# Mixed tokens of 26 tiles kept as fp32, their fp16 halves made in front of the pairs, low rank product in fp32

## The reference

```python
x = x + L0_ffn(L0_cond(x, cond, ...))   # grouped conv of 9 taps + bias; int8 matmul, int32 sums, two scales, fp16
x = x + L1_ffn(L1_cond(x, cond, ...))
# L1_cond: att = softmax(mlp(cond)); out = einsum('boi,bih->boh', agg_w(att), x) + agg_b
# L1_ffn:  H = x W^T + b;  z = x A  (rank 32)
#          logits from H[:, odd tokens, :8] and (z LiMEs^T)[odd tokens], each over its largest magnitude
#          weights = softmax, masked by the second largest;  p_mix = repeat(weights, 2) LiMEs
#          out = H + (z * p_mix) Bmat * scaling
```

## Time and profile before

| | us |
|---|---|
| median of 3 runs | 648.18 |
| span of the profiled execution | 646.6 |
| TensorE busy | 623.8 |
| VectorE busy | 418.3 |
| ScalarE busy | 335.3 |
| GpSimd busy | 336.2 |

### The profile page before, as it was taken

The page is one execution under the profiler, slowest core; times in us unless marked ns, Lnnn a source line. Parts: engine busy times, 40 slices in busy tenths (PEclk is TensorE's granted clock), DMA queues, the critical chain, the costliest instruction groups (busy, mean ns, idle before and its releaser), DMA issues.

```text
span 646.6 us, 14948 instructions
## 1 busy us (share of the span) xinstructions
PE 623.8 (96%) x5865; PEld 337.3 (52%) x5898; DVE 418.3 (65%) x891; ACT 335.3 (52%) x566; POOL 336.2 (52%) x223
## 2 busy tenths in 40 slices
PE   7789999999999999999999999999999999999997
PEld 5556565566566666656554444444444444444443
DVE  5958778877787778787537797745544433444434
ACT  2857898667778777776652436334333313333100
POOL 3012222217778522225485689886866678666400
PEclk8799999999999999999999999999999999999999
DMA  8969877677799797764529014554555433457103
GB/s 299 361 137 365 295 284 273 233 266 276 280 342 336 285 359 280 259 229 140 217 73 357 35 34 153 206 203 156 196 195 193 158 132 136 162 197 259 66 1 130
DMA packets 46707, 138.38 MB, mean 214 GB/s; under 512 B 13180, under 2 KB 13468, under 8 KB 46465
## 3 DMA queue, kind: packets, MB, share of 16 engines
q1 hardware_dynamic: 41886, 120.65, 52.6%
q10 hardware_dynamic: 4752, 16.78, 6.4%
HBM read 89.13 MB, written 48.28 MB: 213 GB/s over the span
## 4 chain that ended last, share of the span: by engine, by line
PE 51%; DVE 1%; issue 0%; ACT 0%; DVEq 0%
PE ps L770 36%; PE ps L584 9%; PE ps L752 2%; PE ps L521 2%; PE ps L505 1%; PE ps L462 0%; PE ps L552 0%; DVE z_lo L1304 0%; DVE unscale L1441 0%; DVE ring L1293 0%; DVE yb L1245 0%; DVE zT L1306 0%; PE ps L555 0%; PE ps L730 0%; PE ps L493 0%
## 5 line engine op out<-in xcount | busy, mean ns | idle before, releaser
L1088 POOL TENSOR_TENSOR x<-x_in,f_both 128x512 f32<-128x512 f32 x64 | 74.0, 1157 | 195.9 <-DVE f_both L1277 195.9
L521 PE MATMUL ps<-wqT,yq_both 128*128 128x512 bf16 x479 | 113.2, 379 | 6.0 <-issue 4.6
L462 PE MATMUL ps<-x_ph,conv_w 64*64 64x256 f32 (+1 forms) x1024 | 98.2, 396 | 2.2 <-DMA conv_w<-in_conv_taps 2.0
L863 ACT ACTIVATE yv<-yb,yinv 128x128 f32<-128x128 f32 x256 | 78.0, 389 | 2.3 <-DVE yinv L1268 2.2
L902 ACT ACTIVATE ring<-ring,ratio 128x2048 f16<-128x2048 f16 x26 | 50.6, 1994 | 51.1 <-DVE wst L1537 14.1
L770 PE MATMUL ps<-ffn_wT,ring 128*128 128x512 f16 x312 | 71.6, 379 | 0.0
L462 PEld LDWEIGHTS ps<-x_ph,conv_w 64*64 64x64 f32 (+1 forms) x1024 | 51.1, 137 | 37.4 <-issue 14.2
L521 PEld LDWEIGHTS ps<-wqT,yq_both 128*128 128x128 bf16 x512 | 45.2, 97 | 48.4 <-issue 1.0
L1245 DVE TENSOR_TENSOR yb<-ps,ybias 128x1024 f32<-128x1024 f32 x32 | 39.1, 1223 | 41.1 <-PE ps L462 41.0
L584 PE MATMUL ps<-ffn_wT,ring 128*128 128x512 f16 x288 | 64.6, 379 | 0.0
L856 ACT ACTIVATE ring<-ps,t_up 128x512 f16<-128x512 f32 x64 | 40.5, 683 | 45.5 <-issue 38.1
(11 more groups left out here) (284 smaller groups left out, 1096.6 us busy)
## 6 DMA issues: line engine op xcount, KB each, us to landing
x_ph<-in_x_phases SPq DMA_DIRECT2D x32, 516.0 KB, 6.1
x_in<-in_x SPq DMA_DIRECT2D x32, 512.0 KB, 6.4
x_scratch<-x SPq DMA_DIRECT2D x32, 512.0 KB, 2.8
x_scratch<-ring SPq DMA_DIRECT2D x26, 512.0 KB, 4.1
ring<-x_scratch SPq DMA_DIRECT2D x26, 512.0 KB, 4.3
wst<-in_w_rows SPq DMA_DIRECT2D x12, 512.0 KB, 5.0
x_in<-x_scratch SPq DMA_DIRECT2D x12, 512.0 KB, 6.5
out<-x_in ACTq DMA_DIRECT2D x12, 512.0 KB, 3.6
```

Of the source, the lines that this page charges most:

```text
L462: return mm(ps_conv[o, g * 2 * MB:(g + 1) * 2 * MB], conv_w[k, g, w.start + o.start:w.start + o.stop], xp[k, g, :, view], start=first, sto ...
L521: last = mm(acc_bank(t, h), yqT[:, t % 2, p, :], wqT[:, p, h * HALF:(h + 1) * HALF], start=p == 0, stop=p == PH - 1)
L863: last = A(yv[:, s, :], yb[:, t % 2, s, :], ACT.Copy, scale=yinv[:, s:s + 1], bias=MAGIC)
L1088: g.tensor_tensor(x1[:, t % 2, s], x_in[:, t % 3, s], f16[:, s], ALU.add).then_inc(sem("x1_ready"), 1)
```

## The change

- Mixed tiles 0 to 25 are kept in the ring and in the scratch tensor as fp32 without a scale. ScalarE copies bank 2 (one instruction in place of two) and no longer waits for the tile's scale; VectorE copies bank 3 (`x2_out`), in front of `layer0(c-2, 0)`. `low` is gone for these tiles. The last six tiles are treated as before.
- Their rank product is made in fp32: 8 matmuls of 40 columns, alternately to partitions 0 and 64, against fp32 weights `z_f`, which ScalarE makes in two instructions before the loop. `rank_out` takes two instructions for two tiles.
- In the last stage `normalized` scales an fp32 tile in place, with the pair's inverse scale; ScalarE rounds the high halves needed (`x_high`: half of the second tile, all of the first) into buffers of their own, three pairs deep, and GpSimd makes the low ones (`x_low`). `x_sums` is gone, and `s_sums` works in the ring in place. `pair` waits for `x_low` where it waited for `normalized`, and `fetch_x2` from the seventh pair tile on waits for `s_low`, where it waited for the end of a pair's products.
- The program is built with a smaller scratch for DMA descriptors, which makes room for the new buffers.

```diff
+x2_sums = ring_flat.rearrange("p (s c t) -> p s c t", s=RING, c=NL)
...
+z_f = sb("z_f", [P, NL, ZR], F32)
+x_part = sb("x_part", [P, 2, L], F32)
...
 def t_home(q):
...
-def x_sum(i):
-    return (bias_b, wsum_b)[i]
+x_homes = ((x_part[:, 0, :], x_part[:, 1, :]), tuple(yb[:, i, :, :].rearrange("p n m -> p (n m)") for i in range(2)),
+           (bias_b[:, :], wsum_b[:, :]))
+
+def x_home(j, i):
+    return x_homes[j % 3][i].bitcast(F16).rearrange("p (a n) -> p a n", a=2)
+
+def x_tile(j, i):
+    return ring[:, x2_slot(RING + 2 * j + i), :]
...
     def save_x2(t):
-        wait(sp, "lo_ready", 2 * t + 2)
+        sp.wait_ge(sem("x2a_ready"), t + 1)
+        sp.wait_ge(sem("x2b_ready"), t + 1)
...
-            sp.wait_ge(sem("prod_ready"), 7 * ((n - 2 * RING) // 2 + 1))
+            sp.wait_ge(sem("s_lo_ready"), 2 * ((n - 2 * RING) // 2 + 1))
...
-        wait(pe, "lo_ready", 2 * t)
+        if t <= KEPT:
+            wait(pe, "x2a_ready", t)
+            wait(pe, "x2b_ready", t)
+        else:
+            pe.wait_ge(sem("lo_ready"), 2 * (t - KEPT))
...
     def rank_pair(t):
-        wait(pe, "lo_ready", 2 * t + 4)
+        if t < KEPT:
+            pe.wait_ge(sem("x2a_ready"), t + 2)
+            pe.wait_ge(sem("x2b_ready"), t + 2)
+        else:
+            pe.wait_ge(sem("lo_ready"), 2 * (t - KEPT) + 4)
...
+            pe.wait_ge(sem("z_f_ready"), 2)
...
+        if t < KEPT:
+            for k in range(NL):
+                o = 64 * (k % 2)
+                last = mm(rank[o:o + ZR, 0:2 * P], z_f[:, k, :], x2_sums[:, s:s + 2, k, :],
+                          start=k < 2, stop=k >= NL - 2, skip_group_check=True)
+            last.then_inc(sem("z_psum"), 1)
+            return
...
-    def x2_part(n, half):
-        return lambda a, k: x2_cols[:, x2_slot(n), a, 4 * half + k, :]
+    def x2_part(j, i, half):
+        return lambda a, k: x_home(j, i)[:, a, (4 * half + k) * P:(4 * half + k + 1) * P]
...
     def pair(j, deltas):
-        n1, n2 = RING + 2 * j, RING + 2 * j + 1
...
-        pe.wait_ge(sem("norm_ready"), 2 * j + 2)
+        pe.wait_ge(sem("x_lo_ready"), 2 * j + 2)
...
-        product(sum_a, x2_part(n1, 0), w_part_of(0, 0), True)
+        product(sum_a, x2_part(j, 0, 0), w_part_of(0, 0), True)
...
     def high(t, h):
...
-            wait(act, "t_ready", 2 * t + 2)
+            if t >= KEPT:
+                act.wait_ge(sem("t_ready"), 2 * t + 2)
...
+        if t < KEPT:
+            if h == 0:
+                A(x2_sums[:, t % RING, :, 0:CH], bank(2).rearrange("p (c t) -> p c t", c=NL), ACT.Copy).then_inc(sem("x2a_ready"), 1)
+            return
...
     def normalized(n):
...
-        act.wait_ge(sem("ratio_ready"), 1)
-        cols = x2_cols[:, s, :, :, :].rearrange("p h c t -> p (h c t)")
-        A(cols, cols, ACT.Copy, scale=ratio[:, t:t + 1]).then_inc(sem("norm_ready"), 1)
+        act.wait_ge(sem("pair_inv_ready"), 1)
+        A(ring[:, s, :], ring[:, s, :], ACT.Copy, scale=pair_inv[:, t:t + 1]).then_inc(sem("norm_ready"), 1)
+
+    def x_high(j):
+        act.wait_ge(sem("norm_ready"), 2 * j + 2)
+        if j == 1:
+            act.wait_ge(sem("gateT_psum"), 1)
+        if j == 2:
+            act.wait_ge(sem("gate_ready"), 1)
+        if j >= 3:
+            act.wait_ge(sem("prod_ready"), 7 * (j - 2))
+        for i, lo in ((1, HALF), (0, 0)):
+            A(x_home(j, i)[:, 0, lo:L], x_tile(j, i)[:, lo:L], ACT.Copy).then_inc(sem("x_hi_ready"), 1)
...
-            act.wait_ge(sem("s_sum_ready"), 6 * j + (4 if i else 6))
-            A(s_home(j, i)[:, :, 0, :], x_sum(i)[:, :].rearrange("p (s n) -> p s n", s=2), ACT.Copy).then_inc(sem("s_hi_ready"), 1)
+            act.wait_ge(sem("s_sum_ready"), 4 * j + (2 if i else 4))
+            A(s_home(j, i)[:, :, 0, :], x_tile(j, i).rearrange("p (s n) -> p s n", s=2), ACT.Copy).then_inc(sem("s_hi_ready"), 1)
...
+    A(z_f[:, :, 0:R], pk[:, PACK["a"]].rearrange("p (k r) -> p k r", k=NL), ACT.Copy, scale=s_up[:, 1:2]).then_inc(sem("z_f_ready"), 1)
+    A(z_f[:, :, R:ZR], pk[:, PACK["w8"]].rearrange("p (k r) -> p k r", k=NL), ACT.Copy, scale=s_up[:, 0:1]).then_inc(sem("z_f_ready"), 1)
...
+    x_high(1)
...
+    x_high(2)
...
-    def x_sums(j):
-        for i in range(2):
-            n = RING + 2 * j + i
-            pool.wait_ge(sem("norm_ready"), n - RING + 1)
-            wait(pool, "s_lo_ready", 2 * j)
-            if n == RING:
-                pool.wait_ge(sem("gate_ready"), 1)
-            hi, lo = (x2_cols[:, x2_slot(n), a, :, :].rearrange("p c t -> p (c t)") for a in range(2))
-            g.tensor_tensor(x_sum(i)[:, :], hi, lo, ALU.add).then_inc(sem("s_sum_ready"), 1)
+    def x_low(j):
+        for i, lo in ((1, HALF), (0, 0)):
+            pool.wait_ge(sem("x_hi_ready"), 2 * j + (1 if i else 2))
+            h = x_home(j, i)
+            g.tensor_tensor(h[:, 1, lo:L], x_tile(j, i)[:, lo:L], h[:, 0, lo:L], ALU.subtract).then_inc(sem("x_lo_ready"), 1)
...
     def s_sums(j):
-        pool.wait_ge(sem("s_sum_ready"), 6 * j + 2)
-        a, b = x_sum(0), x_sum(1)
+        pool.wait_ge(sem("x_lo_ready"), 2 * j + 2)
+        a, b = x_tile(j, 0), x_tile(j, 1)
...
-            wait(pool, "s_sum_ready", 6 * j + 2 + i)
+            wait(pool, "s_sum_ready", 4 * j + i)
...
     def s_low(j):
...
-            g.tensor_tensor(h[:, :, 1, :], x_sum(i)[:, :].rearrange("p (s n) -> p s n", s=2), h[:, :, 0, :], ALU.subtract).then_inc(sem("s_lo_ready"), 1)
+            g.tensor_tensor(h[:, :, 1, :], x_tile(j, i).rearrange("p (s n) -> p s n", s=2), h[:, :, 0, :], ALU.subtract).then_inc(sem("s_lo_ready"), 1)
...
+    def x2_out(t):
+        if t >= KEPT:
+            return
+        dve.wait_ge(sem("mix_ready"), 2 * t + 2)
+        if t >= RING:
+            dve.wait_ge(sem("z_psum"), (t - RING) // 2 + 1)
+            dve.wait_ge(sem(f"x2_moved{t % RING}"), 16 * (t // RING))
+        v.tensor_copy(x2_sums[:, t % RING, :, CH:2 * CH], bank(3).rearrange("p (c t) -> p c t", c=NL)).then_inc(sem("x2b_ready"), 1)
+
     def low(t, h):
-        wait(dve, "hi_ready", 2 * t + h + 1)
+        if t < KEPT:
+            return
+        wait(dve, "hi_ready", 2 * (t - KEPT) + h + 1)
...
     def rank_out(t):
+        if t < KEPT:
+            dve.wait_ge(sem("z_psum"), t // 2 + 1)
+            dve.wait_ge(sem("z_bias_ready"), t // 8 + 1)
+            cols = slice(t * P, (t + 2) * P)
+            link(v.tensor_tensor(z_lo[:, :], rank_bank(t)[64:ZW, 0:2 * P], zT[64:ZW, cols], ALU.add))
+            v.tensor_tensor(zT[0:ZR, cols], rank_bank(t)[0:ZR, 0:2 * P], z_lo[:, :], ALU.add).then_inc(sem("z_ready"), 2)
+            return
...
-            link(v.scalar_tensor_tensor(z_lo[:, :], rank_bank(t)[64:ZW, i * P:(i + 1) * P], t_down[64:ZW, t + i:t + i + 1], zT[64:ZW, cols],
+            link(v.scalar_tensor_tensor(z_lo[:, 0:P], rank_bank(t)[64:ZW, i * P:(i + 1) * P], t_down[64:ZW, t + i:t + i + 1], zT[64:ZW, cols],
...
-                                   z_lo[:, :], ALU.mult, ALU.add).then_inc(sem("z_ready"), 1)
+                                   z_lo[:, 0:P], ALU.mult, ALU.add).then_inc(sem("z_ready"), 1)
...
-        link(v.tensor_scalar(pair_inv[:, :].bitcast(I32), pair_down[:, :].bitcast(I32), -1.0, float(254 << 23), ALU.mult, ALU.add))
-        v.tensor_tensor(ratio[:, :], t_down[:, 0:KEPT], pair_inv[:, :], ALU.mult).then_inc(sem("ratio_ready"), 1)
+        v.tensor_scalar(pair_inv[:, :].bitcast(I32), pair_down[:, :].bitcast(I32), -1.0, float(254 << 23), ALU.mult, ALU.add).then_inc(sem("pair_inv_ready"), 1)
...
+        x2_out(c - 3)
```

More of the change, by code:

```diff
@@ L156, in program @@
         unscale = sb("unscale", [P, NT], F32)
-        z_lo = sb("z_lo", [ZR, P], F32)
+        z_lo = sb("z_lo", [ZR, 2 * P], F32)
         gate_w = sb("gate_w", [ZR, 2 * E], F32)
@@ L170, in program @@
         pair_inv = sb("pair_inv", [P, KEPT], F32)
-        ratio = sb("ratio", [P, KEPT], F32)
         gsm = sb("gsm", [P, 6, NJ], F32)
@@ L578, in dense @@
                         pe.wait_ge(sem("f_ready"), 2 * NT)
-                    pe.wait_ge(sem("lo_ready"), 2 * (KEPT + n) + 2)
+                    pe.wait_ge(sem("lo_ready"), 2 * n + 2)
                     wait(pe, "folded", 2 * n - 3 + h)
@@ L803, in pair @@
                 wait(pe, "pair_folded", 7 * j)
-                product(sum_c, x2_part(n1, 1), w_part_of(1, 0), True)
+                product(sum_c, x2_part(j, 0, 1), w_part_of(1, 0), True)
                 for n in deltas[5]:
@@ L807, in pair @@
                 pe.wait_ge(sem("pair_folded"), 7 * j + 5)
-                product(sum_a, x2_part(n2, 1), t_part(1, 0), False)
+                product(sum_a, x2_part(j, 1, 1), t_part(1, 0), False)
             dense(5, 0)
@@ L1009, in _ @@
             A(gateT, bank(2)[:, 0:P], ACT.Copy).then_inc(sem("gateT_ready"), 1)
+            x_high(0)
             t_high(3)
@@ L1047, in _ @@
                     normalized(2 * j + 11)
+                    x_high(j + 2)
                 store(2 * j + 5)
@@ L1151, in _ @@
             t_sums(3)
-            x_sums(0)
```

(5 more changed lines are left out.)

## The result

The changed kernel takes **657.46 us**, the median of 4 runs (656.20 to 657.74), beside 648.21 us for the kernel before (4 runs on the same chip). The ratio is 1.0139, with a 95% interval of 1.0125 to 1.0153: slower, by 9.2 us or 1.4%. The profiled execution has a span of 655.6 us against 646.6, 9.0 more.

A forecast was written before the change was run, and what follows sets the result against it. TensorE was taken to bound the kernel, busy for nearly the whole span. The terms +5.5 + 7.5 - 2.8 = +10.2, rounded to +10.3, gave a 656.9 us span and, with 1.6 for the median, 658.5 us; range 653.0 to 663.5.

The forecast's parts named there:

- Rank product, +5.5: TensorE's rank product of two tiles takes 1.74 us in fp32 for 1.32, 13 times, wholly on the path: +5.5 us.
- Eviction, +7.5: VectorE's 0.65 us copy before the layer 0 product, against 0.24 us slack: 17 x 0.41 + 7 x 0.08 = +7.5 us.
- Given back, -2.8: Less ScalarE and VectorE work shortens TensorE's waits in iterations 4 to 13: -2.8 us, bounds 0 and 3.6.
- No second delay: Next convolution's third group waits for the layer 0 product's second half, but both move together: nothing added.
- fp32 copies of the rank weights, nothing: About 0.7 us more on ScalarE before iteration 3, covered by its 1.49 us wait for a weight tile: costed at nothing.
- Normalizing and halves, nothing: Last stage: ScalarE's and GpSimd's work for the pairs is covered, pair 0 being 7 us ahead: costed at nothing.
- Median over span, 1.6: The measured median lies 1.6 us above the profiled span, added to turn 656.9 into 658.5 us.
- (a): Rival: VectorE's copy is cheap, at the SBUF rate of 0.37 us; sum +4.9, 653.1 us; chance 0.12.
- (b): Rival: the rank product's fp32 column halves do not run side by side; 28 us in place of 5.5, 681; chance 0.03.
- (c): Rival: the last 11 pairs each wait 1 to 3 us for late halves; 670 to 692; chance 0.04.
- (d): Rival: the fp32 rank product runs at the old 40-column half's rate, 0.45 us for 1.32; 641.5; chance 0.03.
- (e): Rival: VectorE's path has more than 0.24 us slack and over 3 us come back in early tiles; 650.1; chance 0.05.

The follow-up runs named there:

- the late-copy run: The changed kernel with VectorE's copy of the mixed tile moved behind the channel maximum; 650.82 us, ratio 1.0037.

## Why the prediction was right

The forecast was 658.5 us and the result is 657.46, inside the range, by the mechanism forecast for the two cost terms. The term given back came out near its size, but not only by what it was put down to. By the prediction's own terms:

- **Rank product, +5.5.** The step of 0.217 us taken from the convolution held: 16 instructions in 1.76 us from the first start to the next convolution, 0.44 more for a product, 13 x 0.44 = 5.7.
- **Eviction, +7.5.** The place and the slack were right, the copy was over-sized. Its pitch is 0.59 us and not 0.65, so the delay is 0.36 for 0.41; in the seven iterations with one logits product it is 7.90 - 7.87 = 0.03 for 0.08. 17 x 0.36 + 7 x 0.03 = 6.3. I had taken the pitch of a two-source operation with a scale for that of a plain copy. Iteration 3, one of the 17, grew by 0.09 only (10.18 to 10.27). The Trainium skill ("VectorE: DVE Perf Modes", section "Why PSUM operands drop a tier") has fp32 from PSUM at one element a cycle. The traces agree in so far as the copy is far from the SBUF rate: 0.59 us for 512 elements, not 0.37, and 0.59 - 0.33 = 0.26 us for 256 more, not 0.19.
- **Given back, -2.8.** In iterations 4 to 28 the two costs come to 16 x 0.36 + 0.2 + 12 x 0.44 = 11.2 us, and the sum grew by 8.99: 2.2 given back. They lie in iterations 4 to 13, where 9 x 0.36 + 5 x 0.44 = 5.4 became 3.2: measured by these costs iteration 9 gives back 1.2 us, iteration 5 0.55, 10 0.4, 7 0.3 and 11 0.2, and iteration 12 loses 0.5. Iterations 5 and 9 lost their waits for the row sum:

```profile
68.27 0.17 PE L494 MATMUL ps<-x1sum,ones_b 128*128 128x1 bf16 x1
...
106.10 0.17 PE L494 MATMUL ps<-x1sum,ones_b 128*128 128x1 bf16 x1
```

  ScalarE's relief is one part. The other I had not named: a TensorE that comes later finds less to wait for. In both kernels with an added operation iteration 9 became shorter, 10.37 us for 10.73, with none of the relief in them. A third I hadn't seen, since it shows as no idle time of TensorE: in iterations 7 and 11 of the kernel before the convolution itself takes 3.13 and 3.01 us, held for the layer 0 product's second half, and 2.80 in the kernel after. Iteration 7 before, TensorE and VectorE:

```profile
81.63 3.31 PE L462 MATMUL ps<-x_ph,conv_w 128*64 128x256 f32 x32
84.76 1.11 PE L505 MATMUL ps<-mixT,x 64*64 64x64 f32 x64
...
81.89 0.20 DVE L1268 RECIPROCAL yinv<-yscale 128x8 f32<-128x8 f32 x1 [0.45 <-issue]
```

  VectorE is idle for 0.45 us there, in front of the reciprocal and that product, for nothing that the profile shows. The kernel after doesn't have this gap, and no run says why, so 0.3 us of the 2.2 came back by luck. In iteration 11 the convolution is back at 2.80 also in the two kernels that moved `delta_weights` and ScalarE's scalings away.
- **No second delay.** This held by luck, since the reason given is wrong: the product of the second half does not just move along with TensorE. With the copy in the kernel before, the odd convolutions take 3.01 us for 2.80. It costs nothing in the changed kernel, where `low` has gone from in front of that product, and the prediction didn't weigh the one against the other.
- **fp32 copies of the rank weights, nothing.** No stall of TensorE came of them. The start up to iteration 4 scatters by more than their 0.7 us, so the runs can't say more.
- **Normalizing and halves, nothing.** The stretch of the pairs is 247.00 us again. GpSimd makes pair 0's low halves (L1160) and its sums' (L1175) before 394, and the pairs begin at 402:

```profile
375.73 3.24 POOL L1160 TENSOR_TENSOR x_part<-ring,x_part 128x512 f16<-128x512 f32 x2
...
390.47 3.11 POOL L1175 TENSOR_TENSOR yq_both<-ring,yq_both 128x1024 f16<-128x1024 f32 x1
```

  The first pair's product starts at 402.11, so the lead is 402.11 - 393.58 = 8.5 us, where the prediction had read 7.
- **Median over span, 1.6.** It is 657.39 - 655.6 = 1.8 for the profiled kernel's own run, 1.9 by the median.

The span grew by 9.0 us for the 10.3 forecast. The two cost terms were 13.0 and are 12.0, nearly all of it the copy's size; over the whole span 12.0 - 9.0 = 3.0 us came back, 0.8 of them outside iterations 4 to 28, 0.3 in iteration 3 and the rest less than the start's scatter.

Of the rivals, (a), a cheap copy, falls by the pitch of 0.59 and by the late-copy run, which takes 6.6 us away; (b) by the halves run in a row, which shows that they overlap as written; (c) by the 247.00 us; (d) by 1.76 us a product; (e) by even iterations of exactly 8.19 + 0.36. The wait on the channel maximum that I had asked for stands in the even iterations, and iteration 16 takes 8.55 for the 8.6 named.

## What to carry to other kernels

Work taken off an engine is worth nothing where nobody waits for it, and one small operation placed between that engine's wait and its handoff costs its full pitch less the slack, in every iteration in which the slack is that small (here 0.36 us, and 0.03 where a logits product makes room). Read the slack on that handoff (here 0.24 us) before placing anything there, and put work that nobody waits for behind the handoff: one moved line was 6.6 of 9.2 us here. A wait inside a long group of matmuls shows as no idle time, so the length of the group has to be compared too. When an operation is added to a kernel as a probe, it should be of the same kind and read and write the same memories as the one that it stands for.

## What the runs showed of the hardware that was not expected

- Two column halves of TensorE run side by side when their matmuls alternate (8 fp32 matmuls of 40 columns in 1.76 us), and still partly when they come in two blocks of eight instructions: the second block starts 0.90 us after the first, and instructions of one half start before earlier ones of the other.
- A VectorE addition of 512 fp32 from and to SBUF takes 0.68 us, and 1.63 when it begins 1.05 us into GpSimd's two-source operation of 2.13 us; a copy out of PSUM at the same place takes 0.68 always.
